# A Mamba block on one Trainium2 core: chunk-end states in two accumulated stages, and side work moved to other states

## The chip, the cores and the metric

One core of a Trainium2 chip runs the whole program. Its engines are PE (TensorE, matrix products), DVE (VectorE), ACT (ScalarE), POOL (GpSimd) and SP (issues DMAs). The metric is the time of one execution in microseconds; lower is better.

## The reference

A decoder layer: a Mamba block with a residual, then cross attention and a mixture of experts. The change touches the Mamba block alone. For each of 2 layers and 4 sequences of 512 tokens (512 channels, 16 states):

```python
delta = softplus(delta @ dtw + dtb)
dA = exp(delta[..., None] * -exp(a_log))
mi = delta[..., None] * Bm[:, :, None, :] * xb[..., None]
def scan_fn(carry, inp):
    h, v = carry
    v = BETA * v + mi_t          # BETA = 0.6: a filter in time, the same for every channel
    h = dA_t * h + v             # a scan with a decay of its own for every channel and state
    y_t = einsum("ben,bn->be", h, C_t)
y = (ys + dp * xb) * silu(z) ; out = y @ ow
```

## The kernel before

**Items and states.** A layer and a sequence are an *item*: 8 items, k = 0 to 7. An item has 16 states times 4 channel tiles = 64 *steps*; the text calls them states r = 0 to 63 (`i` = 64k + r in the code). Each goes through the engines in a row:

- PE computes the filtered input v of a *pair* of states (L631, 24 products that stand as 48 records): products of the transposed u = delta * x with a small filter, in six chunks of 43 or 42 tokens in each half of the 512. The four 64x64 quarters of the array work at once.
- ACT computes the decay dA (L923), DVE scans (L783), POOL multiplies the scan by C (L987), and PE adds the product into y by transposing (L610), seven states later (LAG = 7).

Buffers tie them: a scan must be done before its PSUM bank is used again; the product of POOL must be there before the transposes of state i - 7; and the products of pair i stand on PE before these.

**Side work.** While item k is scanned, its neighbours are served: the *front* of item k + 1 and the *back* of item k - 1. Each piece stands in `steps[engine][(k, r)]`, and each engine issues it after its own work of state r. Pieces of the front by name: `xn` (transposes), `p` (L515, input projection, and `conv` on DVE, L679), `xp`, `dbcT`, `d`, `clip`, `exp`, `ln`, `max` (softplus in steps, ACT and DVE), `z` (L515, gate projection, copied by ACT), `u` (POOL forms u, L944; PE transposes it, L550; ACT copies it, L885). Of the back: `y`, `bt`, `xd`, `gate` (POOL, L949) and `bo` (L601, output projection).

**Chunk ends.** A chunk needs the value of the filter at the end of the chunk before it. `mid` (L561) sums over the six chunks of the first half for the state in the middle of the sequence; then `c` and `ch` (L569) go from chunk to chunk in five dependent stages, in both halves at once: PE multiplies, ACT copies 16 rows out (L802, in two parts), and the next stage reads them. `bend` holds the weights of these sums, formed on DVE (L691) right behind `bcol`. In item 0 this stands in the opening, before any scan; otherwise at states 50 to 60, one stage every second state.

**Filter pieces.** `pool_filter` (L959) forms the filter of a pair of states; there are 8 for an item, used in states 4p to 4p + 3 and 32 + 4p to 35 + 4p. Before, POOL forms those of item k + 1 at states 34, 38, ... 62 of item k, in 9 buffers.

**Banks.** Six PSUM banks are dealt out in the program's order by `banks_for`: a side piece takes the one left longest; a pair of states takes two neighbouring ones. The plan fixes whom each piece waits for. From the plan: in items 2 to 6, 10 or 11 of the 32 pairs take a bank that the pair right before them has to leave, 54, 56, 58, 60 and 62 among them; in item 1 it is 5 (10, 20, 24, 40, 56).

Of the kernel before, what the change touches and what calls it, by code (L numbers as in the profile page):

```python
# [7 lines left out]
ALU = mybir.AluOpType  # L8
# [7 lines left out]
P = 128  # L16
BETA = 0.6
EPS = 1e-5
NSTATE = 16
# [6 lines left out]
MID = 64  # L26
TILED = ("mid", "c", "ch")
EP, NFILT = 2, 9
# [47 lines left out]
def build(nc, d, out):  # L76
# [14 lines left out]
    with ExitStack() as ctx:  # L91
# [109 lines left out]
        with ExitStack() as mc:  # L201
# [10 lines left out]
            ends = sb(mc, "ends", [P, NCH, 2])  # L212
# [15 lines left out]
            bend = lay(NCH * P).rearrange("p (c n) -> p c n", c=NCH)  # L228
# [47 lines left out]
            def plan_first():  # L276
# [23 lines left out]
                put("dve", "bcol")  # L300
                for m in range(ET):
                    put("pe", "d", m)
                    s += m % 2
                    put("act", "d", m)
# [25 lines left out]
                put("pe", "mid", 0)  # L330
                s += 1
                put("act", "mid", 0)
                for c in range(NCH - 1):
                    s += 1
                    for part in ("c", "ch"):
                        put("pe", part, c)
                    s += 1
                    for part in ("c", "ch"):
                        put("act", part, c)

            def plan_front(k, at, start):
# [3 lines left out]
                p_at = (8, 10, 12, 14) if k > 1 else range(start + 5, start + 5 + ET)  # L345
# [12 lines left out]
                put(23, "dve", "bcol")  # L358
                for m in range(ET):
# [7 lines left out]
                put(32, "act", "ln")  # L367
                put(34, "act", "ln_end")
                for m in range(ET):
                    put(35 + m, "dve", "max", m)  # L370
                    put(36 + m, "pool", "u", m)
                    put(35 + m, "pe", "z", m)
                    put(36 + m, "act", "z", m)
# [3 lines left out]
                put(50, "pe", "mid", 0)  # L377
                put(50, "act", "mid", 0)
                for c in range(NCH - 1):
                    for part in ("c", "ch"):  # L380
                        put(52 + 2 * c, "pe", part, c)
                        put(52 + 2 * c, "act", part, c)

            def plan_back(k, at, s):
# [11 lines left out]
                for t in range(TB):  # L396
                    s = s + 1 if at == "last" else ((17, 19, 21, 23) if at == NI - 1 else (15, 17, 18, 19))[t]
# [5 lines left out]
            def plan_mid(k):  # L403
                for e in range(EP):
# [4 lines left out]
                    steps["pool"].setdefault((k, s + 3), []).append((k, "gate", e))  # L409
# [90 lines left out]
            def pe_side(k, what, j=0):  # L500
# [62 lines left out]
                elif what == "c":  # L563
                    sides = [pe_open(k, part, j) for part in ("c", "ch")]
                    pe.wait_ge(bank_act, emptied_by("act", k, "ch", j - 1) if j else emptied_by("act", k, "mid", 0))
                    for e0 in range(2):
                        for half in range(2):
# [3 lines left out]
                            if e0:  # L571
                                i.then_inc(bank_full, 1)
# [1527 lines left out]
```

## Time and profile before

| | us |
|---|---|
| median of 3 runs | 1558.73 (1557.35 to 1559.39) |
| the profiled execution | 1560.36 |
| its span | 1558.9 |
| first to last product of the states (items 0 to 7) | 78.4 to about 980 |
| mean granted clock of PE | 0.961 of 2.4 GHz |

The Mamba block fills the first two thirds of the span. In it PE, DVE and POOL work side by side on the same states, so none of their busy shares alone is the time. It has to be read item by item and, within an item, by halves: which engine has no idle time left there, and for whom the others wait.

### The profile page before, as it was taken

The page shows a single profiled execution, that of the slowest core. Times are in us where ns is not written, and L with a number is a line of the kernel's source. Part 1 is how long each engine was busy: PE and PEld are TensorE (multiplying, and loading weights), DVE is VectorE, ACT ScalarE, POOL GpSimd, SP SyncE. Part 2 cuts the span into 40 slices and gives each one's busy share as a digit, 9 for nine tenths or more (in the row PEclk, how much of TensorE's full clock was granted, in tenths as well). Part 3 has the DMA queues.
Part 4 walks back from the last instruction along what each step waited for, and adds up shares of the span by engine and source line. Part 5 has one row for each costly group of instructions (what it writes and reads, how often), then busy time and mean ns, then how long its engine had stood idle before and what let it go on. Part 6 is the DMA issues. An engine that isn't in the chain of part 4 may idle for free.

```text
span 1558.9 us, 46788 instructions
## 1 busy us (share of the span) xinstructions
PE 1372.9 (88%) x20442; PEld 975.9 (63%) x20442; DVE 1066.0 (68%) x1347; ACT 908.8 (58%) x1365; POOL 921.2 (59%) x802
## 2 busy tenths in 40 slices
PE   4679799999899899899899886878989887999997
PEld 2357577777677677667677775533444343499996
DVE  4189898798689688788788786577676771422223
ACT  3658567777767667767666765116555655434440
POOL 1159888989979969969969986530303000035541
PEclk8689999999999999999999998969999999999999
DMA  4102212222212212221221344370414100612225
GB/s 134 49 28 85 83 65 75 85 83 96 84 71 84 84 57 84 84 72 69 87 81 70 138 128 125 76 149 1 84 39 85 24 1 15 264 47 69 68 66 179
DMA packets 41497, 127.26 MB, mean 82 GB/s; under 512 B 8784, under 2 KB 21584, under 8 KB 32848
## 3 DMA queue, kind: packets, MB, share of 16 engines
q1 hardware_dynamic: 34736, 108.27, 21.4%
q0 software_dynamic: 6048, 14.95, 3.6%
q8 instruction: 163, 2.67, 0.7%
q10 hardware_dynamic: 512, 1.05, 0.4%
q14 instruction: 38, 0.31, 0.1%
HBM read 97.90 MB, written 9.57 MB: 69 GB/s over the span
## 4 chain that ended last, share of the span: by engine, by line
PE 59%; DVE 20%; issue 10%; ACT 4%; POOL 4%; DMA 2%; DVEq 0%; SPq 0%; ACTq 0%; POOLq 0%
PE psum L631 12%; DVE hst L783 9%; PE psum L610 8%; PE psum L1710 4%; PE psum L1722 4%; PE psum L1298 4%; PE psum L515 3%; POOL hst L987 3%; PE psum L601 3%; DVE overlay L679 2%; PE psum L1280 2%; DVE w_early L783 2%; PE psum L1652 2%; PE psum L1264 2%; DVE nmax L1419 2%
## 5 line engine op out<-in xcount | busy, mean ns | idle before, releaser
L987 POOL TENSOR_TENSOR hst<-hst,cb 128x512 f32<-128x512 f32 x399 | 513.5, 1306 | 125.7 <-DVE hst L783 110.3
L783 DVE TENSOR_TENSOR_SCAN hst<-dA,psum 128x512 f32<-128x512 f32 x399 | 467.1, 1204 | 140.7 <-PE psum L631 140.4
L610 PE MATMUL psum<-ident,hst 128*128 128x128 f32 x1596 | 236.5, 282 | 15.6 <-POOL hst L987 12.7
L610 PEld LDWEIGHTS psum<-ident,hst 128*128 128x128 f32 x1596 | 174.2, 141 | 66.3 <-issue 25.4
L923 ACT ACTIVATE dA<-delta,alog 128x512 f32<-128x512 f32 x256 | 177.0, 718 | 63.1 <-DVE hst L783 43.9
L923 ACT ACTIVATE dA<-xres,alog 128x512 f32<-128x512 f32 x256 | 176.1, 718 | 47.8 <-DVE hst L783 35.6
L1419 DVE TENSOR_REDUCE nmax<-psum 128x2 f32<-128x1024 f32 x128 | 154.6, 1220 | 55.3 <-PE psum L1264 54.8
L1348 ACT ACTIVATE pT<-psum 128x1024 f32<-128x1024 f32 x128 | 128.0, 1024 | 102.9 <-PE psum L1284 79.3
L631 PE MATMUL psum<-filt,c_early 64*64 64x86 f32 (+1 forms) x6144 | 147.2, 241 | 32.8 <-DVE hst L783 23.6
L631 PEld LDWEIGHTS psum<-filt,c_early 64*64 64x64 f32 x6144 | 126.6, 136 | 68.8 <-issue 39.9
L631 PE MATMUL psum<-filt,uT 64*64 64x86 f32 (+1 forms) x6144 | 144.8, 238 | 23.8 <-DVE hst L783 14.6
L631 PEld LDWEIGHTS psum<-filt,uT 64*64 64x64 f32 x6144 | 123.8, 133 | 57.2 <-issue 38.0
L987 POOL TENSOR_TENSOR w_early<-w_early,cb 128x512 f32<-128x512 f32 x113 | 144.5, 1290 | 24.5 <-DVE w_early L783 24.2
L783 DVE TENSOR_TENSOR_SCAN w_early<-dA,psum 128x512 f32<-128x512 f32 x113 | 133.8, 1204 | 30.2 <-PE psum L631 29.9
L1955 POOL DMA_INDIRECT overlay<-x_hat,origin x39 | 37.8, 970 | 186.6 <-DVE c_early L1901 175.1
L515 PE MATMUL psum<-overlay,w_early 128*128 128x512 f32 x256 | 124.4, 614 | 1.9 <-DVE hst L783 1.1
L1961 POOL DMA_INDIRECT y_choice<-yb,goal x39 | 38.5, 986 | 70.0 <-DVE yb L1915 70.0
L1800 ACT ACTIVATE ht<-psum 128x512 f32<-128x512 f32 x39 | 23.3, 597 | 93.9 <-PE psum L1710 93.9
L1710 PEld LDWEIGHTS psum<-xt,xn 128*128 128x128 f32 x624 | 75.6, 192 | 2.8 <-DVE xt L1907 0.9
L1710 PE MATMUL psum<-xt,xn 128*128 128x128 f32 x624 | 76.1, 275 | 0.7 <-DVE xt L1907 0.7
L679 DVE SCALAR_TENSOR_TENSOR overlay<-psum,w_cv,overlay 128x509 f32<-128x509 f32 (+2 forms) x96 | 71.1, 742 | 7.6 <-ACT overlay L823 5.3
L1722 PE MATMUL psum<-w_down,ht 128*128 x312 | 73.7, 380 | 0.0
(236 smaller groups left out, 2130.5 us busy)
## 6 DMA issues: line engine op xcount, KB each, us to landing
cb<-c_rows SPq DMA_DIRECT2D x64, 1024.0 KB, 4.7
qk_first<-w_early SPq DMA_DIRECT2D x64, 64.0 KB, 2.4
qk<-part SPq DMA_DIRECT2D x64, 64.0 KB, 2.7
w_up<-up_dram SPq DMA_DIRECT2D x8, 512.0 KB, 7.3
w_down<-down_dram SPq DMA_DIRECT2D x8, 512.0 KB, 12.9
w_up<-y_choice SPq DMA_DIRECT2D x8, 512.0 KB, 6.9
qk<-part POOLq DMA_DIRECT2D x48, 64.0 KB, 5.2
qk_first<-part SPq DMA_DIRECT2D x40, 64.0 KB, 2.4
```

Source lines behind the costliest of these rows:

```text
L515: i = pe.matmul(bk, w_in[:, kt, m8 * P:(m8 + 1) * P], xnT[:, kt, :], start=kt == 0, stop=kt == KD - 1)
L610: m = pe.matmul(psum[:, Y0 + et % EP, t * P:(t + 1) * P], hst(i)[:, t * P:(t + 1) * P], ident[:], start=n == 0 and t == 0, stop=n == NSTAT ...
L631: m = pe.matmul(halves_at[half][e0:e0 + MT, :, t0:t0 + width], uT[k % 2][r0:r0 + KT, c, et * P + e0:et * P + e0 + MT], filt[r0:r0 + KT, f ...
L679: i = dve.scalar_tensor_tensor(out=dst, in0=bk[:, 0:S - late], scalar=w_cv[:, l, j, tap:tap + 1], in1=dst, op0=ALU.mult, op1=ALU.add)
L783: dve.tensor_tensor_scan(hst(i), a, v, 0.0, ALU.mult, ALU.add).then_inc(scan_done, 1)
L923: act.activation(dA[:, a % NDA, :], delta[k % 2][:, et, :], ACT.Exp, scale=alog[:, k // B, et, n:n + 1]).then_inc(decay_done, 1)
L987: pool.tensor_tensor(h, h, cb[:, q % 2, state_of(i)[1] % GN, :], ALU.mult).then_inc(g_done, 1)
L1298: m = pe.matmul(psum[i * HROW:(i + 1) * HROW, PV, :], vt[:, cp, kv, c0:c0 + HROW], pT[:, (m0 + i // 2) % NPT, i % 2, :], start=kv == 0, st ...
L1348: act.activation(pT[:, m % NPT], pair(u, "score", s), ACT.Exp, scale=HDIM ** -0.5).then_inc(pair_act, 1)
L1419: dve.tensor_reduce(nmax[:, u % 2, t, 2 * j:2 * j + 2], pair(u, "max", r), AX.X, ALU.max, negate=True).then_inc(pair_dve, 1)
L1710: m = pe.matmul(psum[:, U0 + j % NUB, ft * P:(ft + 1) * P], wu[:, j % NWU, kt * F + ft * P:kt * F + (ft + 1) * P], xt[:, j % NXT, kt, :], ...
L1722: m = pe.matmul(out_bank(j)[:, 0:D], ht[:, j % NHT, ft, :], w_down[:, bass.ds(at + ft * D, D)], start=ft == 0, stop=ft == FT - 1)
```

## The change

1. *Chunk ends in two stages.* `lo` sums, for each of the six chunk ends of the first half, over all chunks up to it (1 + 2 + ... + 6 = 21 products); `hi` does the same for five ends of the second half (15 products), once the copies of `lo` are there. Each product has 64 rows, 16 columns of weights and 512 moving columns. Four column strips of the array (`tile_position=(r0, g * BC)`, 32 columns each) take them in turn, with queues of 6, 5, 5, 5 products (`lo`) and 5, 4, 4, 2 (`hi`). Two banks each. ACT copies 6 and then 5 pieces of 16x512 instead of 22 of 16x256. They stand at states 50 and 56. `mid`, `c` and `ch` go.
2. *bend* has 6 x 6 x 16 weights instead of 6 x 2 x 16 and is formed on POOL at state 26 instead of on DVE at 23.
3. *Filter pieces* for item k + 1 at every fifth state from 46: 46, 51, 56, 61, and 2, 7, 12, 17 of item k + 1 itself; 8 buffers.
4. *Other states* for `p` (8, 10, 12, 14 to 6, 9, 12, 14), `z` (35 to 38 to 38, 41, 45, 58), `bo` (15, 17, 18, 19 to 19, 25, 29, 34), the gates of `plan_mid` (40, 42 to 50, 57), `ln`, `max`, `u` on POOL (one or two states earlier). SP issues two loads of C before the reload of weights that waits for the last `z`.

```diff
-TILED = ("mid", "c", "ch")
-EP, NFILT = 2, 9
+LO_AT = ((5, 4, 3, 2), (None, None, 0, 1))
+HI_AT = ((4, 3, 2, 1), (None, None, 0, None))
+TILED = ("lo", "hi")
+EP, NFILT = 2, 8
...
-                p_at = (8, 10, 12, 14) if k > 1 else range(start + 5, start + 5 + ET)
+                p_at = (6, 9, 12, 14) if k > 1 else range(start + 5, start + 5 + ET)
...
+                put(26, "pool", "bend")
...
-                    put(35 + m, "dve", "max", m)
-                    put(36 + m, "pool", "u", m)
-                    put(35 + m, "pe", "z", m)
+                    put(33 + m, "dve", "max", m)
+                    put(34 + m, "pool", "u", m)
+                    put((38, 41, 45, 58)[m], "pe", "z", m)
...
-                put(50, "pe", "mid", 0)
-                put(50, "act", "mid", 0)
-                for c in range(NCH - 1):
-                    for part in ("c", "ch"):
-                        put(52 + 2 * c, "pe", part, c)
-                        put(52 + 2 * c, "act", part, c)
+                for part, s in (("lo", 50), ("hi", 56)):
+                    for n in range(2):
+                        put(s, "pe", part, n)
+                        put(s + n, "act", part, n)
...
-                    s = s + 1 if at == "last" else ((17, 19, 21, 23) if at == NI - 1 else (15, 17, 18, 19))[t]
+                    s = s + 1 if at == "last" else ((17, 19, 21, 23) if at == NI - 1 else (19, 25, 29, 34))[t]
...
-                    steps["pool"].setdefault((k, s + 3), []).append((k, "gate", e))
+                    steps["pool"].setdefault((k, (50, 57)[e]), []).append((k, "gate", e))
...
+                elif what in ("lo", "hi"):
+                    if j:
+                        return
+                    sides = [pe_open(k, what, n) for n in range(2)]
+                    if what == "lo":
+                        pe.wait_ge(bend_done, k + 1)
+                        pe.wait_ge(bank_act, emptied_by("act", k, "u", NCH - 1))
+                    else:
+                        pe.wait_ge(bank_act, emptied_by("act", k, "lo", 1))
+                    at, r0 = (LO_AT, 0) if what == "lo" else (HI_AT, KT)
+                    queues = [[(n, at[n][g], c) for n in range(2) if at[n][g] is not None for c in range(at[n][g] + 1)] for g in range(4)]
+                    for turn in range(NCH):
+                        for g in range(4):
+                            if turn < len(queues[g]):
+                                n, end, c = queues[g][turn]
+                                i = pe.matmul(sides[n][g * BC:g * BC + NSTATE, :], bend[r0:r0 + KT, end, c, :], uT[par][r0:r0 + KT, c, :],
+                                              start=c == 0, stop=c == end, tile_position=(r0, g * BC))
...
-                    if k + 1 < NI and r >= EP * NSTATE and r % (2 * EP) == 2:
-                        pool_filter(NPAIRS * (k + 1) + (r - EP * NSTATE) // (2 * EP))
+                    if i >= PACE0 and (i - PACE0) % TILES % PACE == 0 and (i - PACE0) % TILES < PACE * NPAIRS and (i - PACE0) // TILES + 1 < NI:
+                        pool_filter(NPAIRS * ((i - PACE0) // TILES + 1) + (i - PACE0) % TILES // PACE)
```

What stands on the engines is shown at three places. The names: `filt,c_early` and `filt,uT` are the products of a pair of states (L631, in the new file L627), `ident,hst` and `ident,w_early` the transposes of one state (x4). First PE at states 50 to 54 of item 4, where the chunk ends of item 5 are computed, before:

```order
L631 MATMUL psum<-filt,c_early 64x2x42 x8
L561 MATMUL psum<-uT,overlay 64x256 x12
L610 MATMUL psum<-ident,hst 128x128 x8
L631 MATMUL psum<-filt,c_early 64x2x43 x16
L631 MATMUL psum<-filt,c_early 64x2x42 x8
L569 MATMUL psum<-uT,overlay 64x256 x4
```

and now, from state 50 to 56:

```order
L568 MATMUL psum<-uT,overlay 16x512 x21
L606 MATMUL psum<-ident,hst 128x128 x8
L627 MATMUL psum<-filt,c_early 64x2x43 x16
L627 MATMUL psum<-filt,c_early 64x2x42 x8
L606 MATMUL psum<-ident,hst 128x128 x8
L627 MATMUL psum<-filt,c_early 64x2x43 x16
L627 MATMUL psum<-filt,c_early 64x2x42 x8
L606 MATMUL psum<-ident,hst 128x128 x4
L606 MATMUL psum<-ident,w_early 128x128 x4
L627 MATMUL psum<-filt,c_early 64x2x43 x16
L627 MATMUL psum<-filt,c_early 64x2x42 x8
L568 MATMUL psum<-uT,overlay 16x512 x15
```

The row of 12 products and five rows of 4 behind every pair have become one row of 21 at state 50 and one of 15 at 56; pairs 52 and 54 stand free of them.

PE again, states 19 to 21 of item 4, the output projections of item 3 (`L601`, now `L597`), before:

```order
L610 MATMUL psum<-ident,hst 128x128 x4
L601 MATMUL psum<-overlay,sz 128x256 x4
L610 MATMUL psum<-ident,w_early 128x128 x4
L601 MATMUL psum<-overlay,sz 128x256 x4
L631 MATMUL psum<-filt,c_early 64x2x43 x16
L631 MATMUL psum<-filt,c_early 64x2x42 x8
L610 MATMUL psum<-ident,w_early 128x128 x4
L522 MATMUL psum<-xbs,overlay 64x256 x8
```

and now, one of them at state 25:

```order
L534 MATMUL psum<-dbc,overlay 128x512 x2
L627 MATMUL psum<-filt,c_early 64x2x43 x16
L627 MATMUL psum<-filt,c_early 64x2x42 x8
L606 MATMUL psum<-ident,hst 128x128 x8
L597 MATMUL psum<-overlay,sz 128x256 x4
L534 MATMUL psum<-dbc,overlay 128x512 x2
```

Four output projections that stood at 15 to 19 now stand one at a time at 19, 25, 29 and 34.

POOL, states 9 to 34 of item 5, before (L987 is the product of one state, L949 a gate, L959 a filter piece):

```order
L949 TENSOR_TENSOR xres<-xres,overlay 128x512
L987 TENSOR_TENSOR hst<-hst,cb 128x512
L987 TENSOR_TENSOR w_early<-w_early,cb 128x512 x2
L987 TENSOR_TENSOR hst<-hst,cb 128x512 x7
L987 TENSOR_TENSOR w_early<-w_early,cb 128x512 x2
L987 TENSOR_TENSOR hst<-hst,cb 128x512 x7
L987 TENSOR_TENSOR w_early<-w_early,cb 128x512 x2
L987 TENSOR_TENSOR hst<-hst,cb 128x512 x3
L959 TENSOR_TENSOR filt<-toep,bcol 128x516
```

and now, to state 26 (L954 a filter piece, L934 `bend`):

```order
L944 TENSOR_TENSOR xres<-xres,overlay 128x512
L981 TENSOR_TENSOR hst<-hst,cb 128x512
L981 TENSOR_TENSOR w_early<-w_early,cb 128x512
L954 TENSOR_TENSOR filt<-toep,bcol 128x516
L981 TENSOR_TENSOR w_early<-w_early,cb 128x512
L981 TENSOR_TENSOR hst<-hst,cb 128x512 x4
L954 TENSOR_TENSOR filt<-toep,bcol 128x516
L981 TENSOR_TENSOR hst<-hst,cb 128x512 x3
L981 TENSOR_TENSOR w_early<-w_early,cb 128x512 x2
L981 TENSOR_TENSOR hst<-hst,cb 128x512 x5
L934 TENSOR_TENSOR overlay<-bcol,ends 128x576
```

Filter pieces stand between the products of the first half as well, and `bend` at 26.

## Rows read from the trace of the kernel before

**Rows 1.** The page, part 1: busy us, share of the span, instructions.

```profile
PE 1372.9 (88%) x20442; PEld 975.9 (63%) x20442; DVE 1066.0 (68%) x1347; ACT 908.8 (58%) x1365; POOL 921.2 (59%) x802
```

**Rows 2.** Busy time by stretch: items 0, 1, 2, 6 (first pair to first pair).

```profile
core 0: us, PE busy (x) PEld busy (x) DVE busy (x) ACT busy (x) POOL busy (x), PEclk, DMA share, GB/s
78.40:201.75 123.35, 100.91 (x2116) 76.39 (x2117) 106.44 (x135) 83.62 (x132) 97.34 (x79) 0.92 0.17 62
201.75:310.06 108.31, 104.91 (x2185) 80.16 (x2184) 93.41 (x97) 77.85 (x125) 94.94 (x78) 1.00 0.22 80
310.06:423.31 113.25, 104.27 (x2186) 79.81 (x2185) 94.00 (x97) 81.50 (x137) 104.04 (x85) 1.00 0.24 87
...
764.46:878.59 114.13, 104.56 (x2185) 80.02 (x2185) 93.90 (x97) 78.92 (x125) 99.80 (x81) 1.00 0.22 81
```

**Rows 3.** The same of item 4 by halves: states 0 to 31, 32 to 63.

```profile
537.50:593.85 56.35, 54.30 (x1010) 41.76 (x1009) 51.31 (x59) 39.87 (x64) 42.01 (x35) 1.00 0.21 78
593.85:651.47 57.62, 50.12 (x1176) 38.20 (x1177) 42.58 (x39) 40.72 (x72) 57.25 (x47) 1.00 0.21 76
```

**Rows 4.** PE in order of time, item 4, states 50 to 54: start, us, line.

```profile
627.09 2.76 PE L561 MATMUL psum<-uT,overlay 64*64 64x256 f32 x24
629.78 1.09 PE L610 MATMUL psum<-ident,hst 128*128 128x128 f32 x8
630.80 1.12 PE L631 MATMUL psum<-filt,c_early 64*64 64x86 f32 x48
631.75 0.61 PE L569 MATMUL psum<-uT,overlay 64*64 64x256 f32 x8
632.28 1.09 PE L610 MATMUL psum<-ident,hst 128*128 128x128 f32 x8
634.55 1.12 PE L631 MATMUL psum<-filt,c_early 64*64 64x86 f32 x48 [1.17 <-DVE hst L783]
```

**Rows 5.** The costliest groups of item 4, POOL, states 32 to 63.

```profile
L987 POOL TENSOR_TENSOR hst<-hst,cb 128x512 f32<-128x512 f32 x25 | 32.7, 1329 | 0.5 <-DVE hst L783 0.4
...
L959 POOL TENSOR_TENSOR filt<-toep,bcol 128x516 f32<-128x516 f32 x8 | 8.5, 1064 | 0.0
```

**Rows 6.** The same, PE, states 32 to 63.

```profile
L631 PE MATMUL psum<-filt,c_early 64*64 64x86 f32 (+1 forms) x768 | 17.9, 237 | 7.1 <-DVE hst L783 5.3 <-DVE w_early L783 1.1 <-DVE overlay L712 0.7
```

**Rows 7.** The same, PE, states 0 to 31.

```profile
L631 PE MATMUL psum<-filt,c_early 64*64 64x86 f32 (+1 forms) x769 | 18.2, 237 | 2.0 <-DVE hst L783 2.0
...
L601 PE MATMUL psum<-overlay,sz 128*128 128x256 f32 x32 | 7.6, 379 | 0.0
```

**Rows 8.** PE in order of time, attention: four column strips of 32.

```profile
1104.48 1.07 PE L1298 MATMUL psum<-pT,vt 128*32 128x512 f32 x8
1105.48 0.50 PE L1280 MATMUL psum<-qk_first 64*128 64x512 f32 x2
```

**Rows 9.** Weight loads of these products: ns min/median/max.

```profile
L1298 PEld LDWEIGHTS psum<-pT,vt x512: 106/109/154, 1046.0 to 1308.7; 128*32 128x32 f32 x171
```

**Rows 10.** DVE, item 4: scans and bend.

```profile
L783 DVE TENSOR_TENSOR_SCAN hst<-dA,psum 128x512 f32<-128x512 f32 x51 | 59.8, 1206 | 15.5 <-PE psum L631 15.4
...
L691 DVE TENSOR_TENSOR overlay<-bcol,ends 128x192 f32<-128x192 f32 x1 | 1.4, 1439 | 0.0
```

**Rows 11.** ACT, 560 to 674 us: the copies of chunk ends and of u.

```profile
L802 ACT COPY uT<-psum 16x256 f32<-16x256 f32 x22 | 8.0, 363 | 6.6 <-PE psum L569 3.9 <-PE psum L561 2.5
...
L885 ACT COPY uT<-psum 128x512 f32<-128x512 f32 x6 | 3.2, 589 | 3.4 <-PE psum L550 3.4
```

**Rows 12.** Busy time from the first chunk end to the first pair, item 0.

```profile
58.09:78.40 20.31, 10.86 (x64) 4.82 (x64) 0.00 (x0) 8.01 (x23) 0.00 (x0) 0.51 0.00 1
```

**Rows 13.** PE in order of time, opening.

```profile
14.62 10.17 PE L515 MATMUL psum<-overlay,w_early 128*128 128x512 f32 x16 [0.84 <-DVE overlay L670]
...
58.09 5.21 PE L561 MATMUL psum<-c_early,overlay 64*64 64x256 f32 x24 [1.30 <-ACT c_early L885]
```

**Rows 14.** The page, part 6: loads of C and of the input weights.

```profile
cb<-c_rows SPq DMA_DIRECT2D x64, 1024.0 KB, 4.7
```

More of the change, by code:

```diff
@@ L211, in build @@
             toep = sb(mc, "toep", [P, QC])
-            ends = sb(mc, "ends", [P, NCH, 2])
+            ends = sb(mc, "ends", [P, NCH, NCH])
             keep = sb(mc, "keep", [P, 1])
@@ L300, in plan_first @@
                 put("dve", "bcol")
+                put("pool", "bend")
                 for m in range(ET):
@@ L886, in act_side @@
                              bank(k, "u", j).rearrange("p (c e x) -> p c e x", c=2, e=ET)).then_inc(bank_act, 1)
-                elif what in ("c", "ch"):
-                    act.wait_ge(bank_full, filled(k, "ch", j))
-                    act_carry(uT[par][KT * (what == "ch"):, j + 1, :], bank(k, what, j))
-                elif what == "mid":
-                    act.wait_ge(bank_full, filled(k, "mid", 0))
-                    act_carry(uT[par][KT:, 0, :], bank(k, "mid", 0))
+                elif what in ("lo", "hi"):
+                    act.wait_ge(bank_full, filled(k, what, 1))
+                    for g, end in enumerate((LO_AT if what == "lo" else HI_AT)[j]):
+                        if end is not None:
+                            r0, c = (0 if what == "lo" else KT, end + 1) if end < NCH - 1 else (KT, 0)
+                            i = act.copy(uT[par][r0:r0 + NSTATE, c, :], bank(k, what, j)[g * BC:g * BC + NSTATE, :])
+                    i.then_inc(bank_act, 1)
                 elif what == "x_roots":
@@ L940, in pool_side @@
                 par = k % 2
-                if what == "u":
+                if what == "bend":
+                    pool.wait_ge(bank_dve, emptied_by("dve", k, "dbcT", 0))
+                    if k:
+                        pool.wait_ge(bank_full, filled(k - 1, "hi", 1))
+                    else:
+                        pool.wait_ge(ld_scan, 64)
+                    pool.tensor_tensor(bend, bcol[:, par].unsqueeze(1).to_broadcast([P, NCH, NCH, NSTATE]),
+                                       ends[:].unsqueeze(3).to_broadcast([P, NCH, NCH, NSTATE]), ALU.mult).then_inc(bend_done, 1)
+                elif what == "u":
                     pool.wait_ge(delta_done, ET * k + j + 1)
```

79 lines of the change are left out of this document (23 added, 56 removed).

## The prediction

> **What bounds the kernel now.** The page's busy shares come first, and they decide nothing: PE 88%, DVE 68%, POOL 59% of a span of which the change touches two thirds [rows 1]. So the second view is the busy time item by item [rows 2]. Items 2 to 6 take 113.25 to 114.13 us; their bounds, 310.06 and 878.59, give 568.5 us for five, a mean of 113.7. In each PE is busy for 104.3 to 104.9. Item 1 has the same PE work, 104.91, and takes only 108.31. The third view cuts item 4 in two [rows 3]. In states 0 to 31 PE is busy for 54.30 of 56.35 us: PE sets the pace, with 2.05 idle. In states 32 to 63 PE is busy for 50.12 of 57.62, with 7.5 idle, and POOL for 57.25: there it is POOL that never rests. Its row says the same, 0.5 us of waiting in front of 25 products [rows 5].
>
> Where PE's 7.5 us are is shown in order of time [rows 4]: behind every stage of the chunk ends it waits some 1.15 us for a scan before it can write the next pair (1.17 at 634.55; there are five of these). By the plan of the banks the pairs 54 to 62 take the banks of the pair right before, so that PE and DVE take turns instead of overlapping. The group row has it as 7.1 us in front of L631, 6.4 of them for scans [rows 6]. In item 1 the plan falls better, and the item is 5.4 us shorter than the mean. That is what the trace itself offers as the price of this wait, though POOL's load in that half delays part of it to the next item.
>
> **The change part by part.** The sum is made against the profiled execution (1560.36 us, span 1558.9), 1.6 above the median of the runs.
>
> *Chunk ends, PE.* Removed: `mid`, 627.09 to 629.78 = 2.7 us, and five stages of 0.53 (631.75 to 632.28) = 2.65; together 5.35 [rows 4]. Added: a product is two records, so `lo` has 12 rounds of up to four strips (the longest queue has 6 products) and `hi` 10. What does a round cost? Two bounds. `mid` does 12 rounds of 256 columns on two strips in 2.7 us, 0.224 each, or 0.45 for 512 columns. Attention runs four strips of 32 columns with 512 moving columns: two rounds (x8) and the change of tile behind them take 1.00 us to the next operation, 0.50 a round [rows 8]. I take 0.45, as the change of tile is paid once and not in every round: 22 x 0.45 = 9.9 us; by the other end 11.0. So PE gets 4.5 us more work per item (up to 5.7).
>
> Here a rule speaks against the change. In the attention row the weight loads take 0.109 us each [rows 9], and eight of them with two rounds of columns fit into 1.00 us, so most of them lie beside the products although all strips share their rows. The Trainium skill, "TensorE: Matmul & The Clock Gate", Part 3, says that a weight load overlaps with products in flight only where the row group differs; in `lo` and `hi` all strips have the same rows. By that rule the strips would pay their loads; the rival for it stands below.
>
> *Chunk ends, ACT.* 22 copies, 8.0 us, become 11 of 512 columns; a copy of that width takes 0.59 [rows 11], so 6.5. ACT is busy for 80.6 of 114 us [rows 3] and nothing else changes there: no cost. The copies of `lo` (some 3 us) have pairs 52, 54 and 56 on PE (3 x 2.1, from 627.09 to 634.55 one sees a pair with its transposes as 1.12 + 1.02) before `hi` needs them: hidden. Without that cover they would cost up to 3 us.
>
> *The wait for scans* goes. By the plan of the changed kernel only 5 to 7 pairs of an item still follow their predecessor's banks (24, 26, 46, 48, 50, in odd items 42 and 52 too), and there PE has side work of 2 us and more in between, against two scans of 2.3 us. What is late next is PE itself.
>
> *bend.* 1.44 us leave DVE [rows 10]. On POOL 576 elements, by a filter piece of 516 at 1.06 [rows 5]: 1.2 us, at state 26, where POOL is busy for 42.0 of 56.35 [rows 3]: hidden. It must be there for state 50.
>
> *Filter pieces.* Four of eight, 4 x 1.06 = 4.2 us, move out of the half in which POOL has no rest into the one where it idles 14.3. POOL: 57.25 - 4.2 = 53.0 in the second half, 42.0 + 4.2 + 1.2 = 47.4 in the first. Neither is a bound any more. If they stayed, POOL would hold the second half at 57.2 and eat much of the gain.
>
> *bo, z, p.* One `bo` of 1.9 us (7.6 for four [rows 7]) moves from the first half to the second. The others thin out the stretch of states 16 to 24; their work stays. SP issues two C loads earlier (they take 4.7 us [rows 14] and wait for POOL as before) and the reload of weights after `z` at 58; POOL needs the next C eight states on, 10 us: hidden.
>
> *The sum for an item.* First half, PE: 54.3 - 1.9 = 52.4. Second half: 50.1 + 1.9 + 4.5 = 56.5. Together 108.9. Idle of PE on top: none at best. In item 1, which has few bank waits, it is 108.31 - 104.91 = 3.4 [rows 2]. In item 4 without the five waits of the chunk ends it is 2.05 + 7.5 - 5.7 = 3.85. Item 1 still has some of these waits, and the thinner states 16 to 24 save a part, so I take 2.5: 111.4 us. POOL has 100.5 to do in it and DVE 92.5. During `lo` and the work to the next pair (5.4 + 2.1) DVE has 2.3 us of scans in hand, so it starves for 5 us, and at `hi` for 3 to 4; it has 19 us to spare in an item and POOL 11, so neither costs while PE is the bound.
>
> *The sum for the kernel.* Items 2 to 6: (111.4 - 113.7) x 5 = -11.5. Item 1 loses, since it never had the wait: 111.4 - 108.3 = +3.1. Item 0 has 22 us of idle PE [rows 2] and is bound by DVE (norms of the later sequences); -1 by a shorter `bend` and fewer bank waits, with +-3. Opening: `mid` and `c` take 20.31 us from 58.09 to the first pair, at half clock (granted 0.51) [rows 12]; `mid` alone takes 5.21 there instead of 2.7 [rows 13]. `lo` would need 5.4 us at full clock and 10.8 at half, `hi` 4.5 to 9.0, the copies 3.0 + 2.5, hand-overs some 0.9: 16.3 to 26.2. The 10.17 us of L515 in the opening began slow and ended fast (16 records would need 7.2 at 0.45) [rows 13], and `lo` is as dense: I take 21.3, +1 (ends -4, +6). Item 7 has no front; 0. Sum: -11.5 + 3.1 - 1 + 1 = -8.4, so 1552.0 for the profiled execution and 1550.3 for the median; I say 1550.
>
> **The rivals.**
>
> *More: PE loses all its waits.* 108.9 per item: -24 for items 2 to 6, +0.6 for item 1, -3 and -2 for item 0 and the opening: 1530. For it: PE is never far behind a scan. Against: not even item 1 comes near.
>
> *No change: PE's idle stays as in item 4 without the five waits (3.85), or as in item 1 (3.4).* 112.75 or 112.3 per item: -4.8 or -7.0 for items 2 to 6, +4.4 or +4.0 for item 1: -0.4 or -3.0, so 1556 to 1558. The work added on PE then eats what the wait gave back. For it: both are measured.
>
> *Slower: the waits come back at other pairs.* Pairs 24, 26 and 46 take the banks of the pair before, in every item, 48 and 50 too. If DVE, starved by `lo` and `hi` and then loaded with projections and softplus, is late when PE gets there, three of them cost 1.15 each, as at 634.55 [rows 4], 3.4 us: 114.8 per item, +5.5 for items 2 to 6, +6.5 for item 1, +2.4 for item 0, +1 opening: 1574. It decides where PE has less than 2.3 us of other work between two such pairs. I count 2.1 at 48 and 50, and 2.9 or more at the others; that is against it.
>
> *Slower: the strips pay their weight loads.* 72 records x 0.109 = 7.8 us more per item than at 0.45 a round, in 7 items +55: 1605. Against it: the attention row, where eight loads would have added 0.87 to 0.90 us of columns and only 1.00 passed [rows 8, 9]. The rule of the skill named above is this case.
>
> **How the numbers follow.** Forecast (1545 to 1555.5) 0.45; more 0.15; no change 0.20; waits come back 0.14; weight loads 0.06. A measurement here can tell about 0.2%, 3.1 us, from no change. Faster: forecast and more, 0.60. Same: 0.20. Slower: 0.20. The range leaves out the weight loads, most of the case of 1574 and the end of the case of 1530: 1534 to 1566. The forecast's own range is 1545 to 1555.5.
>
> **What would show it.** In the changed profile: items 1 to 6 of nearly equal length, 111 to 112 us; `lo` as a row of 42 records in 5.4 us and `hi` of 30 in 4.5; no wait for a scan in front of L627 in states 54 to 62; POOL busy for about 53 us of the second half, with idle time right behind `lo`; PE busy for about 109 us of each item. I am wrong if `lo` and `hi` together take over 11 us, if PE idles over 4 us per item, or if POOL shows no idle time in the second half.

## The result, and the profile after

The changed kernel takes 1575.74 us (median of 4 runs, 1572.16 to 1579.03) beside 1558.04 for the kernel before on the same chip: ratio 1.0105, 95% interval 1.0086 to 1.0123. It is slower by 17.7 us, where the forecast had it faster by 8.

Page of the changed kernel, part 1 (answers to [rows 1]):

```profile
span 1577.6 us, 46812 instructions
...
PE 1419.4 (90%) x20506; PEld 977.3 (62%) x20506; DVE 1056.6 (67%) x1339; ACT 895.0 (57%) x1277; POOL 930.5 (59%) x809
```

Busy time by stretch, one row an item from 0 to 7 (answers to [rows 2]; length, PE, PEld, DVE, ACT, POOL, clock):

```profile
82.83:205.12 122.29, 105.37 (x2125) 75.85 (x2125) 104.42 (x134) 82.78 (x121) 94.22 (x76) 0.92 0.18 63
205.12:319.98 114.86, 109.09 (x2193) 79.77 (x2193) 92.63 (x96) 76.79 (x115) 100.37 (x82) 1.00 0.21 76
319.98:433.33 113.35, 109.20 (x2194) 79.63 (x2193) 92.53 (x96) 78.56 (x125) 100.30 (x82) 1.00 0.22 78
433.33:549.11 115.78, 109.44 (x2193) 79.77 (x2192) 92.78 (x96) 78.91 (x125) 100.43 (x82) 1.00 0.23 84
549.11:662.15 113.04, 108.94 (x2193) 79.52 (x2192) 92.54 (x96) 78.56 (x125) 100.32 (x82) 1.00 0.21 77
662.15:777.01 114.86, 109.09 (x2193) 79.57 (x2192) 92.64 (x96) 78.58 (x125) 100.31 (x82) 1.00 0.21 76
777.01:890.06 113.05, 109.44 (x2193) 79.75 (x2193) 92.55 (x96) 76.76 (x115) 100.32 (x82) 1.00 0.23 78
890.06:995.01 104.95, 87.50 (x1858) 72.06 (x1858) 83.61 (x96) 59.26 (x86) 84.29 (x69) 0.92 0.45 132
```

The work came out as forecast: PE is busy for 109 us in every item (108.9 said). What is over it did not: 4.1 us of idle PE in item 4 and 5.8 in item 5, where 2.5 was said. Against the kernel before, the 18.7 us between the spans of the two profiled executions are: opening +4.4, item 0 -1.1, item 1 +6.6, items 2 to 6 together +1.6, item 7 +4.6, all behind it +2.6.

Item 4 by halves (answers to [rows 3]): PE now sets the pace of both, and POOL's bound of the second half is gone.

```profile
549.11:604.60 55.49, 52.41 (x1001) 40.22 (x1000) 50.72 (x56) 40.30 (x65) 49.10 (x41) 1.00 0.21 79
604.60:662.15 57.55, 56.53 (x1193) 39.30 (x1192) 41.82 (x41) 38.26 (x61) 51.22 (x42) 1.00 0.20 76
```

PE and, below it, DVE in order of time, item 5, around the two stages (answers to [rows 4]):

```profile
752.18 5.32 PE L568 MATMUL psum<-c_early,overlay 64*16 64x512 f32 x42
757.43 1.09 PE L606 MATMUL psum<-ident,hst 128*128 128x128 f32 x8
...
763.65 4.46 PE L568 MATMUL psum<-c_early,overlay 64*16 64x512 f32 x30
```

```profile
759.72 4.55 DVE L775 TENSOR_TENSOR_SCAN hst<-dA,psum 128x512 f32<-128x512 f32 x4 [5.02 <-PE psum L627]
```

12 rounds in 5.32 us and 10 in 4.46 are 0.44 us a round, so no strip pays for its weight load (0.09 us each here), and no pair from 54 to 62 waits for a scan. The waits stand elsewhere. All waits of PE in items 4 and 5 (line waited at, by whom it was ended, total, times, longest):

```profile
PE psum L627 <- DVE hst L775: 2.8, 5, 0.8
PE psum L627 <- DVE xm L712: 0.8, 1, 0.8
PE psum L627 <- DVE w_early L775: 0.3, 1, 0.3
PE psum L529 <- ACT dbc L832: 0.2, 1, 0.2
```

```profile
PE psum L627 <- DVE hst L775: 3.1, 6, 0.7
PE psum L627 <- DVE w_early L775: 1.4, 3, 0.8
PE psum L627 <- DVE xbs L704: 1.1, 1, 1.1
```

In both items three of them (0.75, 0.74, 0.58 us) are in front of pairs 14, 18 and 20. In item 4 the rest stand at 28, 40, 48 and 50, in item 5 at 32, 38 to 44, 48 and 50. They are of different sorts. Around pair 18 of item 4, PE and then DVE:

```profile
576.19 1.09 PE L606 MATMUL psum<-ident,hst 128*128 128x128 f32 x8
578.02 1.12 PE L627 MATMUL psum<-filt,c_early 64*64 64x86 f32 x48 [0.74 <-DVE hst L775]
```

```profile
575.55 2.32 DVE L775 TENSOR_TENSOR_SCAN hst<-dA,psum 128x512 f32<-128x512 f32 x2
577.79 2.30 DVE L675 SCALAR_TENSOR_TENSOR overlay<-psum,w_cv,overlay 128x509 f32<-128x509 f32 x3
580.00 5.66 DVE L775 TENSOR_TENSOR_SCAN hst<-dA,psum 128x512 f32<-128x512 f32 x5
```

DVE does not rest there: it has the convolutions of the projections besides the scans, and its scans end 4 to 6 us behind PE. A pair needs two banks, and its own two come free only when both of its scans are done. At each of these three waits five of the six banks hold work that DVE has yet to do; the sixth is one that a projection has left. Of the other waits, the plan explains those at 42, 48 and 50 as the kernel-before's kind: the pair takes a bank of the pair right before (0.35 and 0.33 us, in item 5 also 0.60). At 32, 38 and 40 it takes banks of an earlier pair, with DVE again 4 to 6 us behind. At 28 (0.80 us, the line of `xm`) it takes the bank of a `bo` that the change put at 25 and that DVE has yet to add; at 44 (1.10 us, `xbs`) the bank of a `bt`.

### The profile page after: what moved, and what is told of

The parts are those of the page before. It is cut to its first block, busy times and chain, and to the rows that moved or that the text cites. A ratio compares the mean times of both kernels' runs of the same rounds, so it can differ in the third digit from the quotient of the medians.

```text
span 1577.6 us, 46812 instructions
## 1 busy us (share of the span) xinstructions
PE 1419.4 (90%) x20506; PEld 977.3 (62%) x20506; DVE 1056.6 (67%) x1339; ACT 895.0 (57%) x1277; POOL 930.5 (59%) x809
## 3 DMA queue, kind: packets, MB, share of 16 engines
q1 hardware_dynamic: 34736, 108.29, 21.3%
## 4 chain that ended last, share of the span: by engine, by line
PE 51%; DVE 27%; issue 8%; ACT 7%; POOL 3%; DMA 2%; SPq 2%; DVEq 0%; ACTq 0%
DVE hst L775 12%; PE psum L627 7%; PE psum L568 5%; PE psum L606 5%; PE psum L1704 4%; PE psum L1716 4%; PE psum L1292 4%; DVE overlay L675 3%; DVE w_early L775 3%; PE psum L513 2%; PE psum L1274 2%; POOL hst L981 2%; PE psum L1646 2%; PE psum L1258 2%; DVE nmax L1413 2%
## 5 line engine op out<-in xcount | busy, mean ns | idle before, releaser
L627 PE MATMUL psum<-filt,c_early 64*64 64x86 f32 (+1 forms) x6144 | 146.2, 240 | 20.7 <-DVE hst L775 10.9
L627 PE MATMUL psum<-filt,uT 64*64 64x86 f32 (+1 forms) x6144 | 145.6, 239 | 20.5 <-DVE hst L775 10.5
L627 PEld LDWEIGHTS psum<-filt,c_early 64*64 64x64 f32 x6144 | 125.5, 135 | 58.5 <-issue 42.6
L627 PEld LDWEIGHTS psum<-filt,uT 64*64 64x64 f32 x6144 | 124.8, 134 | 55.7 <-issue 42.0
L1704 PEld LDWEIGHTS psum<-xt,xn 128*128 128x128 f32 x624 | 75.6, 192 | 2.9 <-DVE xt L1901 0.9
```

What stands on the lines that cost most here:

```text
L627: m = pe.matmul(halves_at[half][e0:e0 + MT, :, t0:t0 + width], uT[k % 2][r0:r0 + KT, c, et * P + e0:et * P + e0 + MT], filt[r0:r0 + KT, f ...
L1704: m = pe.matmul(psum[:, U0 + j % NUB, ft * P:(ft + 1) * P], wu[:, j % NWU, kt * F + ft * P:kt * F + (ft + 1) * P], xt[:, j % NXT, kt, :], ...
```

## The experiments

Each run is compared with the kernel before on its own chip (medians 1557.5 to 1561.5). "Item" means from first pair to first pair.

**The change in two parts.**

`chunks_only` is the changed kernel with the states of before for `p`, `ln`, `max`, `u`, `z`, `bo`, gates, filter pieces (`NFILT` 9) and loads of C. `placement_only` is the kernel before with the change's states for them; `mid`, `c`, `ch` and `bend` on DVE stay. The diff of the change shows each line; of `chunks_only` against the changed kernel, for instance:

```diff
-                    put((38, 41, 45, 58)[m], "pe", "z", m)
+                    put(35 + m, "pe", "z", m)
```

> The kernel before with only the chunk ends in two stages and the end weights on GpSimd at state 26; filter pieces, gates, projections, z, bo and softplus where they were. Theory (TensorE bounds every item; the changed kernel lost by idle time that came back at other pairs, by the opening and by item 7): TensorE busy 109 per item, idle about 3 as in the waits of before outside the chunk ends, items 2 to 6 at 112 (1.3 under before, -6), item 1 +3.5, opening +4.4, item 7 as before: 1560, range 1553 to 1566; item 7 at 100 to 101. Rival (the two stages themselves, starving VectorE and GpSimd, cost the time): items at 113 to 115 as in the changed kernel, 1570 or more. Rival (placement was a gain and the stages a loss): over 1576.

> The kernel before with only the moves: filter pieces every fifth state from 46 into the next item, gates at 50 and 57, z at 38, 41, 45, 58, bo at 19 to 34, p, softplus and the strip loads as in the changed kernel; chunk ends in the chained rounds of before, end weights on VectorE. The pairs that take the banks of the pair right before them become 24, 26, 42, 46, 48, 50 besides 54 to 62. Theory: TensorE busy stays near 105, idle grows by 1.5 to 3 per item over before, item 7 +4.6 and what follows it +2.6: 1575, range 1568 to 1585. Rival (the moves are harmless and the stages' work is the whole loss): 1556 to 1560, items at 113. Rival (placement relieves the second half): below 1550.

Measured: stages alone 1567.67, ratio 1.0061 (1.0042 to 1.0080); moves alone 1573.90, 1.0100 (1.0080 to 1.0120). One item (4) of each:

```profile
539.52:651.89 112.37, 108.82 (x2193) 79.59 (x2193) 93.53 (x96) 78.58 (x125) 100.01 (x82) 1.00 0.21 78
```

```profile
544.37:659.03 114.66, 104.47 (x2186) 80.16 (x2185) 93.81 (x97) 80.38 (x135) 99.20 (x81) 1.00 0.21 76
```

The first is just above its range, near the 1570 of its rival; the second came as expected. Both parts lose. The moves add no work to PE (104.5) and still make item 4 0.7 us longer than before, since bank waits come at new pairs on top of four of the five at 54 to 62; item 1, which had few of them, grows by 6.4 us, half of what items 1 to 6 lose (12.7). The waits at 14, 18 and 20 come with the moves: `placement_only` has them (0.57, 0.73, 0.57 us), `chunks_only` does not. But every such edit also deals the banks anew, so neither run shows the work and its place alone. The losses, 9.8 and 16.0 us, do not add up to the 17.7 of both.

**Banks alone.** The oldest-first rule of `banks_for` is replaced by a search over assignments that keeps the 400 cheapest; time is counted in states, and what is late costs its square. No instruction moves.

```diff
-            q = min((b for b in oldest if b + 1 in oldest), key=lambda b: max(oldest.index(b), oldest.index(b + 1)))
+    wait = {"scan": 0, "act": 1.7, "dve": 2.2}
...
+        need = t - 1.0 if scan else t - 0.5
+        left = t + 2.0 if scan else t + wait[who]
...
+                late = max(0.0, max(state[b] for b in take) - need + 1.0)
+                c = cost + late * late
```

> The kernel before with nothing but another assignment of PSUM banks: no pair of products takes the banks of the pair right before it, but for the pair at state 24. Every instruction stays in its order. Theory (what was removed by the change was a wait for banks, not for the chain of copies): the 1.17 us waits of the five rounds go without the rounds, items 2 to 6 come to item 1's 108 from 113 to 114 (-5 to -5.5 each), 1532, range 1526 to 1545. Rival (the rounds wait for their own copies, or the scan of VectorE keeps the pace whatever the banks): 1556 to 1558, no change.

> The changed kernel with nothing but another assignment of PSUM banks: the pairs at 24, 26, 46 and 50 take the banks of the pair right before in each item, in place of five in the even and seven in the odd items. Theory (idle time of TensorE came back through the banks): odd and even items equal at 112 to 113, 1 to 2.5 less in the odd ones and 0 to 1 in the even ones, 1570, range 1565 to 1574. Rival (the work and starved engines set it, not the banks): 1575 to 1577, odd items still 2 us longer than even ones. Rival (banks are nearly all of it): items at 110, below 1560.

The kernel before with these banks: 1532.02, ratio 0.9843 (0.9815 to 0.9871), as its theory said. Its item 4, and all waits of PE in it:

```profile
525.23:631.96 106.73, 104.66 (x2186) 79.87 (x2185) 93.74 (x97) 80.43 (x136) 97.53 (x80) 1.00 0.21 78
```

```profile
PE psum L629 <- DVE overlay L707: 0.8, 1, 0.8
PE psum L659 <- DVE hst L811: 0.7, 1, 0.7
PE psum L578 <- POOL overlay L972: 0.2, 1, 0.2
```

So the wait that the change removes was a wait for banks, and goes without touching the chunk ends. The run also corrects the other half of the reading. The filter pieces stay at their old states here, and the second half of item 4 still falls from 57.62 to 50.76 us; POOL is busy for all of it and takes what is left into the next item. A busy POOL was no bound of that half. The changed kernel gained nothing (1579.34, ratio 1.0139, 1.0117 to 1.0162), a miss: in the even items this assignment has a wait of 2.2 us in front of `bo`, which is its own. So I gave one lag of DVE behind TensorE for each pair, as the trace has it:

> The changed kernel with a third assignment of banks, chosen with the lag of VectorE behind TensorE as the trace has it at each pair (1.3 to 5 us) in place of one lag for all. Theory (the last assignment left bo waiting 2.2 us and the pairs 3 us more; banks that are free when asked for bring idle time to 2 to 3): items at 111 to 112, 1562, range 1556 to 1570. Rival (VectorE and its lag set the idle time whatever the banks are): items at 113 to 115, 1573 or more.

> The kernel before with that third way of assigning banks. Pairs 20, 24 and 52 take the banks of the pair right before. Theory: idle time of TensorE at 1.5 to 3 per item as in the first new assignment (107 to 108.5 per item): 1532 within 4, the same as it. Rival: the wait returns at 20 and 52 for 1 us each, 1540.

1590.61 (1.0198, 1.0172 to 1.0225) and 1549.74 (0.9950, 0.9932 to 0.9968). Both missed: this assignment makes item 0 13 us longer in both (135 and 136), and the items behind are 114 to 118 and 107 to 111. They tell only that an assignment can cost as much as the whole change.

**PE's work.** In `lo` and `hi` only the product of each end's own chunk is left; the kernel leaves out the sums over the earlier chunks.

```diff
-  for c in range(at[n][g] + 1)]
+  for c in (at[n][g],)]
```

> The changed kernel whose two stages run only the product of each end's own chunk, two rounds each in place of 12 and 10; the sums over the earlier chunks are left out, so the chunk ends are not the reference's. TensorE's work falls by 5.32 + 4.46 - 4 x 0.45 = 8.0 us per item, nothing else moves. Theory (TensorE bounds the items): items 1 to 6 from 113 to 115 down to 105 to 108, seven times 7 to 8 less with item 0: 1523, range 1515 to 1535. Rival (GpSimd at 100 of 115 and VectorE, both starved behind the stages, set the items with their own order of work): items stay over 110, above 1545.

1527.11, ratio 0.9803 (0.9777 to 0.9828). Items 4 and 5:

```profile
515.03:622.09 107.06, 102.97 (x2144) 78.09 (x2143) 92.53 (x96) 78.42 (x125) 100.09 (x82) 1.00 0.22 81
622.09:730.97 108.88, 103.11 (x2144) 78.05 (x2143) 92.64 (x96) 78.46 (x125) 100.08 (x82) 1.00 0.22 80
```

PE's busy time fell by 6.0 an item and the item by 6.0 in both; the waits stayed where they were, each within 0.02 us. The two rounds left of each stage take 1.9 us in place of the 0.9 that I counted, so it is 6.0 and not 8.0. DVE and POOL have the same to do as in the changed kernel: in these items PE's work and its waits are the bound, POOL's 100 is not.

**Filter pieces at the old states.**

```diff
-EP, NFILT = 2, 8
+EP, NFILT = 2, 9
-            FEARLY, PACE0, PACE = 3, 46, 5
+            FEARLY = 3
```

and the condition for `pool_filter` of before.

> The changed kernel with filter pieces at the states of before (every fourth from 34, none in items' first halves, NFILT 9) and all else as changed. First theory, as read from the two profiles (the four pieces in item 7's first states hold up its gates and so the end): item 7 from 105 back to 101, items 1 to 6 unchanged, 1571. What the last runs speak for (item 7 was 106.4 with the pieces at the old states too): item 7 unchanged at 104 to 106, 1575 within 3. Rival (the new pace relieves GpSimd in the second half and is a gain): 1579 or more.

1572.14, ratio 1.0091 (1.0066 to 1.0115); item 7 takes 101.4 (105.0 in the changed kernel), items 1 to 6 are as they were. Waits of PE for POOL in item 7, changed kernel and then this one:

```profile
PE psum L606 <- POOL hst L981: 10.3, 2, 8.8
...
PE psum L606 <- POOL w_early L981: 1.2, 1, 1.2
```

```profile
PE psum L606 <- POOL hst L981: 7.7, 1, 7.7
...
PE psum L606 <- POOL w_early L981: 0.9, 1, 0.9
```

The first theory holds here: in this kernel the four pieces in the states 2 to 17 of item 7 go with some 3.5 us. The size does not carry over: `placement_only` has these pieces too and takes 102.0, `chunks_only` has none and takes 106.4, and below, in `before_banks`, they add 1.0 (104.0 to 105.0). What sets item 7 is open; each is one execution, and the granted clock there changes between executions too (see the last section).

**The place of bo.**

`old_bo` is the changed kernel with this line; `before_banks_bo` has it the other way round, in `before_banks`.

```diff
-((17, 19, 21, 23) if at == NI - 1 else (19, 25, 29, 34))[t]
+((17, 19, 21, 23) if at == NI - 1 else (15, 17, 18, 19))[t]
```

> The changed kernel with the four bo products and their adds back at states 15, 17, 18, 19 (the change has 19, 25, 29, 34); all else as changed. The trace of the changed kernel has VectorE without rest and its scans 4 to 6 us behind TensorE at states 8 to 20, and TensorE waiting 0.75, 0.74 and 0.57 us there for a scan whatever the bank assignment was. Theory (these states are VectorE's, and TensorE's 7.6 us of bo were free there; the change moved them to states that TensorE bounds): the three waits go, even items 111, odd ones 112 to 113, about 2 us less in each of six, 1563, range 1557 to 1568. Rival (TensorE's total alone counts, wherever its pieces stand): no change, 1573 or more. Rival (the adds behind bo hold up VectorE at states 15 to 20 as much as they free TensorE): 1573 or more, with TensorE's waits at 10 to 20 still there.

> The kernel before with the first new bank assignment, and the four bo products and their adds at 19, 25, 29, 34 as in the change; nothing else is moved. Pairs 24 and 26 take the banks of the pair right before. Theory (bo was free beside VectorE's load at states 8 to 20): items at 108.5 to 110 in place of 107 to 108, TensorE waiting for scans at 10 to 18, 1532 + 6 x 2 = 1544, range 1538 to 1549. Rival (the place of bo is nothing): 1532 within 3.

`old_bo`: 1577.16 (1.0112, 1.0088 to 1.0136), a miss: the wait at 20 went, that at 14 stayed, at 18 there was one of 0.92 us for the add behind a `bo` (the second rival), and a new bank wait of 2.2 us stood before a `z` (1.7 in item 2). `before_banks_bo`: 1540.46 (0.9863, 0.9841 to 0.9885); six items are together 657.5 us in place of 646.6, 1.8 each, with PE waiting 1.09 us for a scan at 18. That is the size expected, but the two ratios' intervals overlap, so for the whole kernel the loss is not shown.

**Before, once more.**

> The kernel before, unchanged, a second look: how far the opening (first pair at 78.4), item 7 (100.4, granted clock 0.95) and what follows it (580.0) repeat. The opening was 76.2 to 82.8 and item 7 101.4 to 106.4 in the kernels that change neither. If item 7's 105.0 and the opening's 82.8 are the change's doing: 78.4 within 1 and 100.4 within 1 again. If both move with the execution: either differs by 2 or more.

1559.53 beside 1561.54. First pair at 78.8, item 7 100.55, the items within 0.4 us of [rows 2], behind item 7 578.1 (580.0). They repeat. Over the kernels that share it, though, the opening is 75.6 to 79.9 with the chained chunk ends (8 executions) and 78.0 to 86.4 with the two stages (9, `one_round` at 69.9 left out), means 77.7 and 81.5; the time behind item 7 is 575 to 583 in all of them, in no order.

**Banks fitted to each kernel's own trace.** Before these, the stages were also run with the first search:

> The kernel with the chunk ends in two stages and nothing moved (as in the run of the stages alone, 1567.7) with the first new bank assignment; pairs 24 and 50 take the banks of the pair right before. It stands to the kernel before with that assignment (1532.0) as the price of the stages alone. Theory (TensorE bounds the items, its work grows by 4.2 to 4.5 each): items at 111 to 112 with TensorE idle 2 to 3, 1532 + 6 x 4.4 = 1558, range 1553 to 1564. Rival (two stages pay once banks are free, as fewer hand-overs between TensorE and ScalarE): 1540 or less. Rival (stages starve VectorE and GpSimd for 4 to 5 us at a stretch and cost more than their work): 1566 or more, idle 4 or more.

1579.28 (1.0112, 1.0085 to 1.0139), a miss. Item 4 has a bank wait of 1.78 us that is the assignment's own, and a stop of 1.98 us in the middle of pair 46, for which the profile shows no releaser (see the last section). So the assignment was then searched against the times at which each product and its taker stand in the kernel's own trace, and written out as a table `BANKS`, one digit for each use in the order of `rows` (846 in the kernel before, 790 in the others):

```diff
-    for name, who in todo:
+    for (name, who), q in zip(rows, BANKS):
```

> The kernel before, every instruction in its order, with banks fitted to a trace: by that trace no product of items 1 to 7's first states would still wait for a bank (the kernel before has 8.2 to 8.5 us of such waits in items 2 to 6 and 2.3 in item 1, the first new assignment 1.2 to 1.8). Theory (TensorE's work of 104.7 bounds the item, all idle time is bank waits): items 1 to 6 at 105 to 106.5, 1522, range 1514 to 1530. Rival (VectorE at 94 and GpSimd at 98 of 107 with their own waits hold the item at 107): 1529 or more.

> The two stages alone (nothing moved), with banks fitted to that kernel's trace: 0.55 us of bank waits left per item, from 3.4. Theory: TensorE 108.8 to 109.1 and idle under 1.5: items at 109.7 to 110.5, 1546, range 1540 to 1556; against before_fit +4.3 per item and so +22 to +30 in all. Rival (the stages starve VectorE for 5.0 and 3.8 us each and it can't catch up, so new waits come): items at 112 or more, 1562 or more.

> The changed kernel with banks fitted to its own trace: 2.3 us of waits left in even items and 3.0 in odd ones, from 3.1 to 3.7 and 5.3; those left are for VectorE's scans at states 14, 18, 20 (0.7, 0.7, 0.55), where every bank holds work that VectorE has not done. Theory: items at 111.3 and 112.1, 1560, range 1554 to 1567; against chunks_fit +1.5 to +2.5 per item, the price of the moves (bo's products taken from VectorE's stretch). Rival (moves are free once banks are fitted): the same as chunks_fit within 3.

Measured side by side: 1536.03 (0.9838, 0.9809 to 0.9867), 1571.41 (1.0072, 1.0047 to 1.0097), 1574.11 (1.0093, 1.0067 to 1.0119). Item 4 of the first two:

```profile
521.62:627.84 106.22, 105.25 (x2186) 80.24 (x2185) 93.52 (x97) 80.39 (x136) 97.37 (x80) 1.00 0.21 77
```

```profile
550.29:662.86 112.57, 110.02 (x2193) 79.95 (x2192) 93.33 (x96) 78.71 (x125) 99.88 (x82) 1.00 0.21 78
```

and the waits left in the second:

```profile
PE psum L548 <- POOL overlay L939: 1.7, 1, 1.7
PE psum L627 <- DVE hst L775: 0.3, 1, 0.3
PE psum L597 <- DVE hst L775: 0.3, 1, 0.3
```

Each was slower than expected. The bank waits went as fitted, but others came: for POOL at state 44 (1.7 us; it has yet to form `u`, with filter pieces among its work), and stops of 0.5 to 2.0 us at 46 with no releaser shown. In `after_fit` those at 14, 18 and 20 stayed, as expected. What is left is the difference. With the banks fitted to each, the stages alone cost 35.4 us. Over items 1 to 6 that is 5.8 each (651.4 and 686.0 us), of which PE's busy time is 4.4 and idle 1.4. The size hangs on the banks: with oldest-first in both the stages cost 9.8 us, with the first search in both 44 (each against its own kernel before). PE's 4.4 us of new work an item is common to all three; the rest is waits and clock. The moves (after_fit against chunks_fit) cost 2.7 us, which the intervals do not tell from none, and items 1 to 6 are together 5.7 us shorter with them (680.3); the 1.5 to 2.5 an item that I expected is refuted.

**The pace of the filter pieces, with banks out of the way.** `before_banks` with the change's `NFILT`, `PACE0` and `PACE`.

> The kernel before with the first new bank assignment (1532.0 alone) and the change's filter pieces: every fifth state from 46 into the next item, NFILT 8. Theory (the pieces at 34, 38 and 42 hold up GpSimd's products for the state transposes at 44, where items 3 and 6 wait 1.1 to 1.4 us for it; the pieces in item 7 cost 3.5): items at 106.5 to 107.5, that is 1 less in three of them, item 7 +2 to +4: 1532, range 1528 to 1537, no wait for GpSimd at 44. Rival (the pieces in an item's first half hold up GpSimd where VectorE and it are both full, and the gates with them): items at 108 or more, 1540 or more.

1529.57 beside 1561.38: ratio 0.9788 (0.9761 to 0.9815), the fastest full kernel of the study. Whether the pace adds to the banks (0.9843, 0.9815 to 0.9871) is just short of shown. No wait for POOL at 44, as said, but items 1, 2 and 5 stop for 0.7 to 1.6 us at 46, with no releaser shown, and the six items sum to 646.7, exactly as without it; the profiled execution is shorter in its opening and item 0.

## Why the prediction was wrong, step by step

- *What bounds the kernel: right for PE, wrong for POOL.* PE idled for banks behind every stage of the chunk ends; `before_banks` takes the waits away alone and gets 5.7 us an item back in items 2 to 6 (568.5 to 539.9 us). The step "that is what the trace itself offers", 5.4 by item 1 [rows 2], was sound. That POOL would hold the second half at 57.2 us if the filter pieces stayed was not: `before_banks` leaves them there and has 50.8.
- *Rounds of 0.45 us: right* (0.44), as was 4.5 us of new PE work, the copies of ACT hidden, `bend` and filter pieces in the items (POOL 51.2 in the second half for 53.0). DVE starved for the 5 us said; that this costs nothing is not shown, since with fitted banks the stages bring 1.4 us of idle PE beside their work. The Trainium skill says that a weight load overlaps with products in flight only where the row group differs ("TensorE: Matmul & The Clock Gate", Part 3). By that rule `lo` and `hi` would have paid some 7.8 us (the prediction's estimate); the trace disagrees: the rows of 42 and 30 records show none of it for strips in different columns.
- *Idle 2.5 us an item: the step that failed.* I took item 4's 3.85 without the five waits as an upper end and went below it, for a stretch that was thinned out. It was 3.6 to 4.2 (even items) and 5.8 to 6.3 (odd). 2.1 of it is mostly the moves' doing, at pairs 14, 18 and 20, where DVE is full; the prediction had these moves save time there. The rest is bank waits at 28 to 50. Nor did the stages alone reach 2.5: in `chunks_only` PE idles 3.6 us in item 4 and 4.4 in item 5. This term alone is 1.1 to 3.8 us in each of six items: 11.5 of the 13.1 us by which items 2 to 6 miss their sum, and 3.3 of item 1's 3.5. The rival "waits come back at other pairs" gave 1574 and had 0.14. Waits did come back, but that its number is right is luck: of its pairs 24, 26 and 46 did not wait and 48 and 50 waited for 0.35 us, not 1.15, and it had the opening at +1 and item 7 at 0.
- *Item 1 +3.1:* it was +6.6, for the same term. The forecast's gain hung on its five neighbours having 5.4 us to lose; PE's new work took 4.5 of that at once, and 0.9 was left to pay for every other miss. That balance was in the sum, and I gave it 0.60.
- *Opening +1:* +4.4 in the traces, +3.8 between the means of the two kinds of kernel. 1.4 of the 4.4 lies ahead of `lo`, which starts at 59.48 for 58.09. From there to the first pair it is 23.35 us where I had 21.3: `lo` took 7.90 us, with a granted clock of 1.00 for its first 2.5 us and 0.50 behind, and `hi` 8.69 at 0.50 throughout, where I had let the clock come back in between.

```profile
59.48 7.90 PE L568 MATMUL psum<-c_early,overlay 64*16 64x512 f32 x42 [1.30 <-ACT c_early L871]
71.11 8.69 PE L568 MATMUL psum<-c_early,overlay 64*16 64x512 f32 x30 [3.72 <-ACT c_early L878]
```

- *Item 7, "0":* +4.6. I counted the pieces of item 7's filters as free since POOL has room in a first half. Without them the same kernel has 3.5 us less there (`old_pace`), but with them `placement_only` is only 1.6 us above the kernel before, so the cause of the 4.6 is open. The last 2.6 us, behind item 7, stay open too; other kernels scatter as much there.

Together: of the 27.1 us between the forecast (-8.4) and the spans (+18.7), idle PE in items 1 to 6 is 14.8, item 7 4.6, the opening 3.4, the end 2.6, and 1.7 is the rest.

## What to carry to other kernels

When an engine waits for a buffer that rotates, ask first whether another order of the same buffers ends the wait; here that was worth 26 us, and restructuring the work that stood next to it cost 18. A stretch that was bounded by waits has room for new work on the engine only until the waits are gone: put the new work and the old waits in one sum, and price the idle time that is left at what the kernel shows now, not below. And where buffers are dealt in the program's order, moving a piece deals them all anew: `bo` moved away cost 1.8 us an item with searched banks, and moved back in the changed kernel it brought nothing.

## What the runs showed of the hardware

The granted clock can fall after one wait of about 2 us in the middle of dense work. In `old_bo`, item 4, behind 2.20 us of waiting:

```profile
611.10 2.40 PE L513 MATMUL psum<-overlay,w_early 128*128 128x512 f32 x4 [2.20 <-DVE hst L775]
613.30 1.06 PE L606 MATMUL psum<-ident,hst 128*128 128x128 f32 x4
...
617.48 0.60 PE L591 MATMUL psum<-ident,xraw 128*128 128x128 f32 x4
```

Four transposes take 1.06 us and, 4 us later, four take 0.60; the granted clock is 0.50 from 613.3 to 615.0 (1.2 GHz) and 1.00 from 617.5 on (2.4 GHz). The same in `chunks_banks`: the stretch behind the wait of 1.78 us and the one with the stop of 1.98 have a granted 0.90 and 0.89, and PE's busy time of that item is 112.1 in place of 108.8:

```profile
599.84:617.00 17.16, 17.16 (x245) 11.70 (x245) 14.72 (x14) 14.00 (x21) 17.09 (x13) 0.90 0.18 64
617.00:631.92 14.92, 12.95 (x357) 11.00 (x356) 10.71 (x11) 6.57 (x11) 14.92 (x14) 0.89 0.21 72
```

It does not always: of the five items of `old_bo` with a wait of 2.2 us it falls in three (1, 4 and 6), and items 3 and 5 have a clock of 1.00. The changed kernel's 6 to 11 waits an item, none over 1.1 us, leave it at 1.00. Nor does it need a wait: in `before_fit`, item 5, PE has none in the 10 us before the clock falls, and its last work there is small, 24 products of 32x32 (0.89 us) and then these of 32 rows:

```profile
673.26 1.73 PE L537 MATMUL psum<-dbc,overlay 32*128 32x512 f32 x4
674.92 1.77 PE L632 MATMUL psum<-filt,uT 64*64 64x86 f32 x48
```

The pair takes 1.77 us for 1.12, and the granted clock is 0.50 from 675.2 to 678.6.

The stops at state 46 I had not expected either. The kernel before has them too (1.09 us at 621.16 in item 4). The traces point to the loading of instructions. In `chunks_banks` a packet of 16 KB on the queue of kind `instruction` runs from 625.1 to 626.0, inside pair 46, and PE stands from 625.56 to 627.54. In items 1 to 6 of all 18 traces PE has 54 stops over 0.4 us without a releaser; 45 of them, and all over 0.8 us, end 1.2 to 2.0 us behind the end of such a packet, where a moment taken at random lies in about one case of eight. No run here tests it.

Item 7 shows the clock as well: it is 0.95 in the kernel before and 0.92 in the changed one, and PE's busy time there 84.3 and 87.5 us for the same work. In a second execution of the kernel before it was 86.8 at 0.93 with the item as long (100.55), so the clock is not by itself the length of item 7.
